# Moving a set of weight loads and their splits within the second of four batch groups

## The chip, the cores and the metric

The kernel runs on one core of a Trainium2 chip. The metric is device time in microseconds. One execution is also profiled; all rows below come from its trace, and their times count from the start of its span.

## What is computed

The input `x` is 32 samples of 64 channels and 1024 positions. Two layers follow each other, each with its own residual:

```
c  = conv(x, 9 taps, 4 channel groups) + (cond @ c_weight.T)[:, :, None] + bias
x  = x + c @ W.T + bias + (per-sample LoRA of c, rank 16)
m  = per-sample 64x64 mix of channels, weights = softmax(MLP(cond)) over 8 matrices
     applied to x, plus a mixed bias
s  = m @ Wr.T                      # 64 experts
G  = softmax over the 16 best of s, zero elsewhere
x  = x + 2 * ((m @ A_k.T) * G_k) @ B_k, summed over the 64 experts k, rank 16
```

With 64 experts of rank 16 the last line is two 1024x1024 products with the gates between them.

## The kernel before

The 32 samples are worked in four groups of eight (`g` = 0 to 3). A group has 512 tokens of 1024 elements, as four tiles of 128 rows. Every float32 matmul operand is split into a high part (a copy by ScalarE, `..._hi`) and a low part (the rest, a subtraction by VectorE, `..._lo`), and a product is three matmuls: high by high, high by low, low by high (`product`, L1374 to L1376).

Weights stream through four slots (`piece_hi`, `piece_lo`, piece n in slot n % 4). A piece of 512 KB comes in one of two ways. A *raw* piece is loaded to `raw` (two buffers) by SP (`next_raw`, L316), and split by ScalarE (L647) and VectorE (L893). Raw n can be loaded only when VectorE has split the raw piece two places before it. A *kept* piece was computed once, split, and stored in DRAM (`kept`); `fetch` loads both parts of it (L344, L345).

The first layer and the last product of groups 1 to 3 are done with seven block products instead of eight, and these need sums of weight blocks. There are four sets of such sums ("units" 0 to 3). For each, `load_weights` loads four blocks of 512 KB (L371), `combine` makes the sums in place on VectorE (L999 to L1006), `combined_hi` (ScalarE, L711) and `combined_lo` (VectorE, L1012) split them, and `keep_weights` stores each of the four splits with two DMAs of 512 KB (L378, L379). Sets 0 to 2 are made in group 0, set 3 in group 1, in the space of `conv_in` (the sums) and `u_hi`, `u_lo` (the splits). So `conv_in` can be loaded for group 2 only when the set's splits are done, and `u_hi` can take gated values of chunks c and c+1 only when the stores of that part have landed (`s_comb`).

A group goes through these stages on TensorE: the convolution (L1388), the first layer as products on pieces 0 to 13 with LoRA between them (L1395 to L1402), the mixing (L1408) and the scores (L1414, L1415) with the first h product among them, and the h stage. In the h stage product `h_of(c)`, here h0 to h7, uses raw piece 14 + c and writes one of the banks 2, 3, 6, 7, 4, 5, 2, 3. TensorE transposes the scores after the first part of h1 (`score_transposed`, L1431) and the gates after h2 (L1438). VectorE picks the 16 best (`choose`), and ScalarE stores the gates and spreads them back over the partitions, four DMAs of 256 KB (L699) ahead of split 21, four more as buffers come free. Then `gated` (L988) multiplies bank c by its gates; `u_hi`, `u_lo` take the split. After the h stage come products on pieces 22 to 35.

The order on each engine and queue is written out by hand, and each runs its own in order. In group 1, VectorE has the splits of raw pieces 17 to 21 and then the `gated` items, ScalarE has split 16, the exponentials of the gates, splits 17 and 18, the copy and store of the gates (`gates_out`), splits 19 and 20, `spread_gates`, split 21 and the gated chunks. SP has raw 16 and 17, the stores of set 3, raw 18, four loads of `conv_in` (L319), raw 19 to 21, two broadcasts of biases, raw 22. TensorE waits in h6 and h7 for the `gated` item that frees their bank:

```
if c >= 6 and ks[0] == 0:
    pe.wait_ge(s_item, g * ITEMS + H0 + c - 5)
```

Of the kernel before, what the change touches and what calls it, by code (L numbers as in the profile page):

```python
# [69 lines left out]
def adaln_ffn_kernel(nc, conv_x, x, taps, pieces, first_consts, hidden_w, later_consts, lora_a, lora_b,  # L70
                     starts, wr, expand, spread, out):
    with ExitStack() as ctx:
# [241 lines left out]
        def _(sp):  # L314
            def load_raw(r, piece):
                sp.dma_start(raw[:, r % RAWS, :], pieces[piece]).then_inc(s_raw[r % RAWS], 16)  # L316

            def load_conv_in(g, t):
                sp.dma_start(conv_in[:, 2 * t:2 * t + 2].rearrange("p b g q -> p (b g q)"),  # L319
                             conv_x[bass.ds(g, 1), t].rearrange("a p n -> (a p) n")).then_inc(s_convin[t], 16)  # L320
# [20 lines left out]
            def fetch(g, n):  # L341

                step_used(sp, g, n - SLOTS)
                sp.dma_start(piece_hi[:, n % SLOTS, :].bitcast(F32), kept[KEPT[n], 0]).then_inc(s_fetched[n % SLOTS], 16)  # L344
                sp.dma_start(piece_lo[:, n % SLOTS, :].bitcast(F32), kept[KEPT[n], 1]).then_inc(s_fetched[n % SLOTS], 16)  # L345

            def lo_done(r_lo):

                sp.wait_ge(s_piece_lo, r_lo)
# [129 lines left out]
            def group(g, last):  # L479
                def next_raw(n):  # L480

                    r = RAW_AT[n]
                    lo_done(g * RAWS_G + (3 + r))
                    load_raw(r, RAW[n % STEPS])

                fetch(g, 4)
                next_raw(8)
                fetch(g, 5)
                next_raw(9)
                if g == 1:  # L490
                    for i in range(4):
                        sp.wait_ge(s_comb_in[i], 48)
                        load_weights(3, i)
                fetch(g, 6)
                fetch(g, 7)
                next_raw(14)
                fetch(g, 10)
                next_raw(15)
                for n in range(11, 14):
                    fetch(g, n)  # L500
                next_raw(16)
                next_raw(17)
                if g == 1:
                    for step in range(4):
                        keep_weights(3, step)
                elif not last:
                    load_conv_in(g + 1, 0)
                    load_conv_in(g + 1, 1)
                next_raw(18)
                if g == 1:  # L510
                    load_conv_in(g + 1, 0)
                    load_conv_in(g + 1, 1)
                if not last:
                    load_conv_in(g + 1, 2)
                    load_conv_in(g + 1, 3)
                for n in range(19, 22):
                    next_raw(n)
                if not last:
                    cond_bias(g)
                    mix_bias(g)  # L520
                next_raw(22)
                next_raw(23)
                if g == 1:
                    for i in range(4):
                        sp.wait_ge(s_comb[i], 32 * 4)
                next_raw(26)
                next_raw(27)
                fetch(g, 24)
                fetch(g, 25)
                fetch(g, 28)  # L530
                next_raw(32)
                fetch(g, 29)
                fetch(g, 30)
                next_raw(33)
                fetch(g, 31)
                for t in range(2):
                    store(g, t, 0, 5 + t)
                if not last:
                    next_raw(STEPS)
                fetch(g, 34)  # L540
                if not last:
                    next_raw(STEPS + 1)
                fetch(g, 35)
                if not last:
                    next_raw(STEPS + 2)
                for t in range(2):
                    store(g, t, 1, 15 + t)
                if not last:
                    next_raw(STEPS + 3)
                    next_x(g, 0, 0)  # L550
                for t in range(2):
                    for h in range(2):
                        store(g, 2 + t, h, 21 + 2 * t + h if last else 18 + 3 * t + h)
                if not last:
                    for th, h in ((1, 1), (0, 1), (1, 0)):
                        next_x(g, th, h)

            first_group()
            for g in range(1, GROUPS):
                group(g, g == GROUPS - 1)  # L560
# [77 lines left out]
        def _(act):  # L638
# [51 lines left out]
            def gates_out(g, bank):  # L690
                act.wait_ge(s_gate_t, g + 1)
                act.activation(gate_t, banks[bank][0:KR_E, :], ACT.Copy).then_inc(s_gate_hi, 1)
                act.wait_ge(s_gate_hi, g + 1)
                act.dma_start(gates, gate_t).then_inc(s_gates_out, 16)
# [12 lines left out]
            def combined_hi(unit, step):  # L707

                i = (0, 1, 3, 2)[step]
                act.wait_ge(s_comb_sum, 4 * unit + step + 1)  # L710
                act.activation(kept_hi(unit, i), raw_weights(unit, i), ACT.Copy).then_inc(s_comb_hi, 1)  # L711
# [115 lines left out]
            def group(g, last):  # L827
                def next_split(n):

                    step_used(act, g, n - SLOTS)  # L830
                    split_raw(g, n)

                for b in range(GB):
                    conv_hi(g, b)
                    if b == 1:

                        act.wait_ge(s_conv, g * GB + 1)
                        split_raw(g, 3)
                first_product(g, 0, (4, 5))
                sums_hi(g, 0)  # L840
                lora_parts(g)
                next_split(8)
                next_split(9)
                next_split(14)
                next_split(15)
                for i, c in enumerate(CHUNKS):
                    split_hi(g, MIX0 + i, v_hi[:, c, :], work[:, c, :])
                    if g == 1 and i % 2 == 0:
                        combined_hi(3, i // 2)
                score_out(g, 5)  # L850
                next_split(16)
                gates_exp(g)
                next_split(17)
                next_split(18)
                gates_out(g, 0)
                next_split(19)
                next_split(20)
                act.wait_ge(s_gates_out, 16 * g + 16)
                for c in range(GATES):
                    spread_gates(c)  # L860
                next_split(21)
                for c in range(NCH):
                    if g == 1 and c % 2 == 0:
                        act.wait_ge(s_comb[c // 2], 32 * 4)
                    gated_hi(g, c)
                    if c == 1:
                        next_split(22)
                    if c == 3:
                        next_split(23)
                next_split(26)  # L870
                first_product(g, 1, (6, 7))
                next_split(27)
                sums_hi(g, 4)
                next_split(32)
                next_split(33)
                if not last:
                    next_split(STEPS)
                    next_split(STEPS + 1)
                    next_split(STEPS + 2)
# [6 lines left out]
        def _(dve):  # L886
            dve.wait_ge(s_ones, 4)

            def split_raw(g, n):

                r = RAW_AT[n]
                dve.wait_ge(s_piece_hi, g * RAWS_G + (5 + r))
                dve.tensor_tensor(piece_lo[:, n % SLOTS, :], raw[:, r % RAWS, :],  # L893
                                  piece_hi[:, n % SLOTS, :].bitcast(F32), ALU.subtract).then_inc(s_piece_lo, 1)
# [113 lines left out]
            def combined_lo(unit, step):  # L1008

                i = (0, 1, 3, 2)[step]  # L1010
                dve.wait_ge(s_comb_hi, 4 * unit + step + 1)
                dve.tensor_tensor(kept_lo(unit, i), raw_weights(unit, i), kept_hi(unit, i).bitcast(F32),  # L1012
                                  ALU.subtract).then_inc(s_comb_lo, 1)
# [160 lines left out]
            def group(g, last):  # L1174
# [102 lines left out]
                for i, c in enumerate(CHUNKS):  # L1277
                    mix_item(g, i, c, (6, 7, 4)[i % 3])
                    if i:
                        mix_lo(g, i - 1, CHUNKS[i - 1])  # L1280
                    if g == 1 and i % 2:
                        combined_lo(3, i // 2)
                mix_lo(g, NCH - 1, CHUNKS[-1])
                split_raw(g, 16)
                choose(g, 1)
                for n in range(17, 22):
                    split_raw(g, n)
                dve.wait_ge(s_lo, g * ITEMS + H0)
                for c in range(0, 6, 2):
# [509 lines left out]
```

## Time and profile before

| | us |
|---|---|
| median of three runs | 658.17 |
| lowest and highest | 656.51, 658.33 |
| the profiled execution | 656.7 |
| its span | 654.9 |
| TensorE busy | 648.1 (99%) |
| VectorE busy | 451.4 (69%) |
| ScalarE busy | 214.0 (33%) |
| DMA, mean rate | 241 GB/s |

Busy time of TensorE is modelled at the ends of matmuls, so 99% says that it has nearly no gaps. The mean granted clock is 0.999 of full speed. Group 1 runs from 178.8 to 337.6 us, group 2 from there to 494.5 us.

### The profile page before, as it was taken

The numbers are of one execution on the slowest core, as the hardware profiler recorded it, in microseconds if no ns is written. First come the engines' busy times: TensorE is split into PE (matmuls) and PEld (weight loads), VectorE is DVE, ScalarE is ACT, GpSimd is POOL, SyncE is SP. The second block draws the span as 40 slices with busy tenths as digits, with TensorE's granted clock in tenths as the row PEclk, the third lists the DMA queues.
The fourth block names the chain that finished last, engine by engine and source line by source line (L and its number), as shares of the span: only waits on it lengthen the run. The fifth ranks groups of instructions, "written<-read, shape, count | busy, mean of one in ns | idle before, by whom it ended". The sixth has DMA issues, their size and how long they took to land.

```text
span 654.9 us, 8354 instructions
## 1 busy us (share of the span) xinstructions
PE 648.1 (99%) x3197; PEld 537.7 (82%) x3197; DVE 451.4 (69%) x690; ACT 214.0 (33%) x275; POOL 73.8 (11%) x91
## 2 busy tenths in 40 slices
PE   9999999999999999999999999999999999999997
PEld 8878888888897788888889788888879888888885
DVE  2859469549377788558769758636967856665785
ACT  2714135233144024335115312333423421433420
POOL 1598200000000160000000042000000000000000
PEclk9999999999999999999999999999999999999999
DMA  8587714986969926776976682287797664037795
GB/s 303 210 293 279 299 50 144 356 246 218 392 228 379 356 100 260 280 223 245 366 275 220 261 318 97 102 225 245 290 325 264 273 248 184 0 118 203 211 345 221
DMA packets 51594, 157.98 MB, mean 241 GB/s; under 512 B 5488, under 2 KB 6384, under 8 KB 51568
## 3 DMA queue, kind: packets, MB, share of 16 engines
q1 hardware_dynamic: 46240, 148.05, 62.7%
q10 hardware_dynamic: 5328, 9.61, 4.8%
q8 instruction: 13, 0.21, 0.1%
q14 instruction: 13, 0.11, 0.1%
HBM read 131.94 MB, written 25.71 MB: 241 GB/s over the span
## 4 chain that ended last, share of the span: by engine, by line
PE 91%; DVE 3%; DMA 3%; issue 1%; SPq 1%; ACT 0%; DVEq 0%
PE bank L1374 25%; PE bank L1376 24%; PE bank L1375 24%; PE bank L1388 9%; PE bank L1408 3%; DMA piece_lo<-kept 2%; PE bank L1395 2%; PE bank L1414 1%; PE bank L1402 1%; PE bank L1400 1%; PE bank L1415 1%; DVE x L925 1%; DMA gate<-hidden_w 1%; DVE u_lo L1012 1%; DVE work L932 1%
## 5 line engine op out<-in xcount | busy, mean ns | idle before, releaser
L893 DVE TENSOR_TENSOR piece_lo<-raw,piece_hi 128x1024 fp32r<-128x1024 f32 x60 | 74.1, 1239 | 90.0 <-ACT piece_hi L647 89.8
L647 ACT ACTIVATE piece_hi<-raw 128x1024 fp32r<-128x1024 f32 x60 | 63.4, 1058 | 147.1 <-PE bank L1376 103.2
L1374 PE MATMUL bank<-piece_hi,u_hi 128*128 128x512 f32 x272 | 107.9, 397 | 0.0
L1376 PE MATMUL bank<-piece_hi,u_lo 128*128 128x512 f32 x272 | 107.3, 395 | 0.0
L1375 PE MATMUL bank<-piece_lo,u_hi 128*128 128x512 f32 x272 | 107.3, 394 | 0.0
L1374 PE MATMUL bank<-v_hi,piece_hi 128*128 128x512 f32 x256 | 101.8, 398 | 0.0
L1376 PE MATMUL bank<-v_hi,piece_lo 128*128 128x512 f32 x256 | 101.1, 395 | 0.0
L1375 PE MATMUL bank<-v_lo,piece_hi 128*128 128x512 f32 x256 | 101.0, 394 | 0.0
L1374 PE MATMUL bank<-piece_hi,v_hi 128*128 128x512 f32 x192 | 76.0, 396 | 0.8 <-DMA piece_lo<-kept 0.8
L1376 PE MATMUL bank<-piece_hi,v_lo 128*128 128x512 f32 x192 | 75.8, 395 | 0.0
L1375 PE MATMUL bank<-piece_lo,v_hi 128*128 128x512 f32 x192 | 75.8, 395 | 0.0
L652 ACT ACTIVATE u_hi<-work 128x512 fp32r<-128x512 f32 x64 | 40.1, 631 | 87.6 <-DVE work L988 50.8
L925 DVE TENSOR_TENSOR x<-x,bank 128x512 f32<-128x512 f32 x86 | 54.3, 679 | 17.0 <-PE bank L1402 12.7
L1374 PEld LDWEIGHTS bank<-piece_hi,u_hi 128*128 128x128 f32 x272 | 51.2, 188 | 12.4 <-issue 0.5
L1376 PEld LDWEIGHTS bank<-piece_hi,u_lo 128*128 128x128 f32 x272 | 51.2, 188 | 12.0
L1375 PEld LDWEIGHTS bank<-piece_lo,u_hi 128*128 128x128 f32 x272 | 51.2, 188 | 11.8
L1388 PE MATMUL bank<-toep,conv_in 128*128 128x128 f32 x512 | 59.2, 276 | 0.2 <-DMA toep<-taps 0.2
L1388 PEld LDWEIGHTS bank<-toep,conv_in 128*128 128x128 f32 x512 | 58.2, 192 | 0.8 <-DMA toep<-taps 0.4
L1376 PEld LDWEIGHTS bank<-v_hi,piece_lo 128*128 128x128 f32 x256 | 48.2, 188 | 11.5
L1375 PEld LDWEIGHTS bank<-v_lo,piece_hi 128*128 128x128 f32 x256 | 48.2, 188 | 11.0
L1374 PEld LDWEIGHTS bank<-v_hi,piece_hi 128*128 128x128 f32 x256 | 48.2, 188 | 10.9
L899 DVE TENSOR_TENSOR u_lo<-work,u_hi 128x512 fp32r<-128x512 f32 x64 | 43.7, 686 | 15.1 <-ACT u_hi L652 13.8
(143 smaller groups left out, 800.7 us busy)
## 6 DMA issues: line engine op xcount, KB each, us to landing
raw<-pieces SPq DMA_DIRECT2D x76, 512.0 KB, 5.5
piece_hi<-kept SPq DMA_DIRECT2D x48, 512.0 KB, 4.7
piece_lo<-kept SPq DMA_DIRECT2D x48, 512.0 KB, 5.8
x<-x SPq DMA_DIRECT2D x16, 512.0 KB, 5.3
gate_x<-gates ACTq DMA_DIRECT2D x32, 256.0 KB
out<-x SPq DMA_DIRECT2D x32, 256.0 KB, 4.8
conv_in<-conv_x SPq DMA_DIRECT2D x15, 516.0 KB, 7.1
conv_in<-pieces SPq DMA_DIRECT2D x12, 512.0 KB, 8.8
```

The costliest lines, as they stand in the source:

```text
L647: act.activation(piece_hi[:, n % SLOTS, :], raw[:, r % RAWS, :], ACT.Copy).then_inc(s_piece_hi, 1)
L652: act.activation(to, of, ACT.Copy).then_inc(s_hi, 1)
L893: dve.tensor_tensor(piece_lo[:, n % SLOTS, :], raw[:, r % RAWS, :], piece_hi[:, n % SLOTS, :].bitcast(F32), ALU.subtract).then_inc(s_piece ...
L899: dve.tensor_tensor(to, of, hi, ALU.subtract).then_inc(s_lo, 1)
L925: dve.tensor_tensor(half, half, of, ALU.add).then_inc(done, 1)
L932: dve.tensor_tensor(work[:, c, :], banks[bank][:, :], mixb_bc[:, :, :].rearrange("p b c -> p (b c)"), ALU.add).then_inc(s_item, 1)
L1374: pe.matmul(to, left_hi, right_hi, start=first, stop=False)
L1375: pe.matmul(to, left_hi, right_lo, start=False, stop=False)
L1376: return pe.matmul(to, left_lo, right_hi, start=False, stop=last)
L1388: mm = pe.matmul(banks[bank][:, cg * P:(cg + 1) * P], conv_in[:, b, cg, h:h + Q], toep[:, cg, 1 - h, :], start=(h == 0), stop=(h == 1))
L1395: mm = pe.matmul(banks[bank][0:LORA_M, :], lora_a_r[:, k, :], part[:, k, :], start=(k == 0 and part is u_hi), stop=(k == NCH - 1 and part ...
L1408: mm = pe.matmul(banks[bank][:, t * P:(t + 1) * P], x1[:, t, c * P:(c + 1) * P], blockdiag[:, t, :], start=True, stop=True)
```

## The change

In group 1, SP issues `fetch` 6 and 7 ahead of the four loads of set 3, no longer behind them. The splits of set 3 leave the mixing: `combined_hi` comes on ScalarE after split 18, ahead of `gates_out`, and `combined_lo` on VectorE after split 18, ahead of split 19. On SP the stores of set 3 follow them: raw 18, 19 and 20 go first, then the eight stores, then the four loads of `conv_in`, then raw 21. Groups 0, 2 and 3 keep their order.

```diff
@@ sp, group @@
                 next_raw(9)
+                fetch(g, 6)
+                fetch(g, 7)
                 if g == 1:
                     for i in range(4):
                         sp.wait_ge(s_comb_in[i], 48)
                         load_weights(3, i)
-                fetch(g, 6)
-                fetch(g, 7)
                 next_raw(14)
...
                 next_raw(17)
                 if g == 1:
+                    for n in range(18, 21):
+                        next_raw(n)
                     for step in range(4):
                         keep_weights(3, step)
-                elif not last:
-                    load_conv_in(g + 1, 0)
-                    load_conv_in(g + 1, 1)
-                next_raw(18)
-                if g == 1:
-                    load_conv_in(g + 1, 0)
-                    load_conv_in(g + 1, 1)
-                if not last:
-                    load_conv_in(g + 1, 2)
-                    load_conv_in(g + 1, 3)
-                for n in range(19, 22):
-                    next_raw(n)
+                    for t in range(4):
+                        load_conv_in(g + 1, t)
+                    next_raw(21)
+                else:
+                    if not last:
+                        load_conv_in(g + 1, 0)
+                        load_conv_in(g + 1, 1)
+                    next_raw(18)
+                    if not last:
+                        load_conv_in(g + 1, 2)
+                        load_conv_in(g + 1, 3)
+                    for n in range(19, 22):
+                        next_raw(n)
@@ act, group @@
                     split_hi(g, MIX0 + i, v_hi[:, c, :], work[:, c, :])
-                    if g == 1 and i % 2 == 0:
-                        combined_hi(3, i // 2)
...
                 next_split(18)
+                if g == 1:
+                    for step in range(4):
+                        combined_hi(3, step)
                 gates_out(g, 0)
@@ dve, group @@
                         mix_lo(g, i - 1, CHUNKS[i - 1])
-                    if g == 1 and i % 2:
-                        combined_lo(3, i // 2)
...
                 choose(g, 1)
-                for n in range(17, 22):
+                split_raw(g, 17)
+                split_raw(g, 18)
+                if g == 1:
+                    for step in range(4):
+                        combined_lo(3, step)
+                for n in range(19, 22):
                     split_raw(g, n)
```

## Rows read from the trace of the kernel before

**Rows 1.** The page, busy microseconds, share of the span and instructions of each engine.

```profile
PE 648.1 (99%) x3197; PEld 537.7 (82%) x3197; DVE 451.4 (69%) x690; ACT 214.0 (33%) x275; POOL 73.8 (11%) x91
```

**Rows 2.** TensorE's waits: who waited for what, us in total, times, longest.

```profile
PE bank L1374 <- DMA piece_lo<-kept: 0.8, 1, 0.8
PE bank L1414 <- DVE v_lo L899: 0.5, 2, 0.3
```

**Rows 3.** TensorE's timeline, groups 1, 2: start, us, instruction, idle before it.

```profile
204.10 0.40 PE L1395 MATMUL bank<-u_hi,lora_a_r 128*112 128x512 f32 x1
...
214.36 0.47 PE L1374 MATMUL bank<-piece_hi,v_hi 128*128 128x512 f32 x1 [0.79 <-DMA piece_lo<-kept]
...
363.01 0.39 PE L1395 MATMUL bank<-u_hi,lora_a_r 128*112 128x512 f32 x1
...
372.31 0.39 PE L1374 MATMUL bank<-piece_hi,v_hi 128*128 128x512 f32 x1
```

**Rows 4.** Windows of TensorE, mixing: length, busy (records), clock, DMA share, GB/s.

```profile
240.50:259.01 18.51, 17.90 (x108) 1.00 0.61 240
398.38:415.77 17.39, 17.39 (x108) 1.00 0.25 91
```

**Rows 5.** Timeline of SP's queue, first layer of group 1: start and us of the issue.

```profile
200.04 2.17 SPq L371 DMA_DIRECT2D conv_in<-pieces  x4
...
202.77 0.45 SPq L345 DMA_DIRECT2D piece_lo<-kept  x1
```

**Rows 6.** Windows of all engines: busy times, then clock, DMA share and GB/s.

```profile
198.46:213.56 15.10, 15.10 (x65) 11.67 (x64) 11.14 (x12) 6.81 (x8) 0.00 (x0) 1.00 1.02 406
...
277.00:279.40 2.40, 2.40 (x12) 1.97 (x11) 0.00 (x0) 0.00 (x0) 0.00 (x0) 1.00 0.99 306
279.40:290.00 10.60, 10.60 (x47) 8.57 (x47) 4.89 (x6) 3.39 (x4) 0.00 (x0) 1.00 0.82 229
```

**Rows 7.** TensorE's timeline: score transposes, first matmul of h6, first of product 22.

```profile
259.01 0.49 PE L1431 MATMUL bank<-consts,small 128*128 128x128 f32 x3
...
287.12 0.39 PE L1374 MATMUL bank<-v_hi,piece_hi 128*128 128x512 f32 x1
...
298.28 0.40 PE L1374 MATMUL bank<-piece_hi,u_hi 128*128 128x512 f32 x1
```

**Rows 8.** VectorE's timeline, h stage of group 1: splits 17, 18, 19, 20, first gated item.

```profile
266.38 2.35 DVE L893 TENSOR_TENSOR piece_lo<-raw,piece_hi 128x1024 fp32r<-128x1024 f32 x2
273.38 2.52 DVE L893 TENSOR_TENSOR piece_lo<-raw,piece_hi 128x1024 fp32r<-128x1024 f32 x2 [4.65 <-ACT piece_hi L647]
...
281.72 0.68 DVE L988 TENSOR_TENSOR work<-bank,gate_x 128x512 f32<-128x512 f32 x1
```

**Rows 9.** ScalarE's timeline in the same stage: copy of the gates, split 21.

```profile
270.59 0.59 ACT L692 ACTIVATE small<-bank 64x512 f32<-64x512 f32 x1 [5.20 <-PE bank L1438]
...
279.49 1.06 ACT L647 ACTIVATE piece_hi<-raw 128x1024 fp32r<-128x1024 f32 x1 [4.84 <-DMA raw<-pieces]
```

**Rows 10.** SP's queue in the same stage: loads of conv_in, raw 19 and 20, raw 21.

```profile
261.02 2.12 SPq L319 DMA_DIRECT2D conv_in<-conv_x  x4
267.62 1.46 SPq L316 DMA_DIRECT2D raw<-pieces  x2
...
274.64 0.33 SPq L316 DMA_DIRECT2D raw<-pieces  x1
```

**Rows 11.** Group 2: ScalarE's queue spreads the gates, VectorE's wait for the fourth.

```profile
430.44 2.52 ACTq L699 DMA_DIRECT2D gate_x<-gates  x4
...
447.85 0.69 DVE L988 TENSOR_TENSOR work<-bank,gate_x 128x512 f32<-128x512 f32 x1 [0.74 <-DMA gate_x<-gates]
```

**Rows 12.** Window of TensorE after its last matmul, columns as in rows 4.

```profile
652.00:654.90 2.90, 0.00 (x0) 0.86 0.68 251
```

**Rows 13.** TensorE's timeline: the first matmuls of the kernel, the convolution of group 3.

```profile
0.99 5.09 PE L1370 MATMUL bank<-ones 128*128 128x128 f32 x24 [0.99 <-POOL ones L566]
...
494.30 14.45 PE L1388 MATMUL bank<-toep,conv_in 128*128 128x128 f32 x128
```

## Prediction

> **What bounds the kernel now.** I read the page's busy times first: TensorE is busy for 99% of the span [rows 1], so nothing but its own work and its few stalls sets the end. The change touches no matmul. It can give back stalls, or make new ones. The waits of TensorE come next: one wait on a transfer, of `piece_lo<-kept`, lasts 0.8 us [rows 2]; the others are smaller and lie at the start or in the mixing.
>
> The four groups run one after another, and groups 1 and 2 issue the same matmuls, so group 2 is a ruler for group 1. From the first LoRA matmul to the start of product 6 to 7, TensorE's timeline has 214.36 - 204.10 = 10.26 us in group 1 and 372.31 - 363.01 = 9.30 us in group 2 [rows 3]: 0.96 us lost, in one place. From the first mixing matmul to the score transposes it is 18.51 us against 17.39 us, both of 108 records [rows 4]: 1.12 us lost. This is all that the change can win, 2.1 us or 0.3% (about what a measurement of this kernel can tell from no change).
>
> **Part 1, the loads go behind fetches 6 and 7.** The issues on SP's queue show the stall's cause. Four loads of 512 KB are issued at 200.04 us, the low half of piece 6 at 202.77 us [rows 5], and it is used at 214.36 us, 11.6 us later. In this stretch the queue moves 406 GB/s [rows 6], so 512 KB (0.524 MB) take 1.29 us and the four loads 5.2 us. Without them in front, piece 6 lands some 5 us earlier, against a need of 0.96 us. The stall goes whole. Next in line is piece 7, which loses its four predecessors too. The loads themselves then land in the place of the two fetches, at about 217 us; the sums that read them (L999) come on VectorE at 222 us, a cover of some 4 us. If it were gone, VectorE and not TensorE would wait first. Gain 0.96 us.
>
> **Part 2, the mixing loses four splits.** VectorE has four `combined_lo` between the mix items, and the scores wait for its `v_lo` there, two waits of 0.5 us in sum and the rest spread over slower steps [rows 2]. ScalarE's four `combined_hi` leave with them. Group 2 without them shows the gain, 1.12 us. Part of it may stay lost: the first of the two waits lies ahead of all four splits, behind work that isn't changed. I take 0.94 us, between 0.7 and 1.1. Parts 1 and 2 together: -1.9 us (1.7 to 2.1).
>
> **Part 3, the splits in the h stage.** I count from M, the start of the score transposes, 259.01 us in group 1 [rows 7]. VectorE ends the splits of pieces 17 and 18 at 266.38 + 2.35 = M+9.7 and starts that of 19 at 273.38 = M+14.4 [rows 8]. Four splits at 2.35 / 2 = 1.18 us take 4.7 us, from M+9.7 to M+14.4. They fill the idle time exactly and delay piece 19 by nothing, which TensorE needs only for h5, one h product of 5.6 us ahead of h6, at M+22.5 [rows 7]. The four on ScalarE lie ahead of its copy of the gates, where it idles 5.20 us for TensorE's transposes [rows 9]. So the engines' work costs 0, with a cover of 7 us on TensorE's side once split 19 is done.
>
> **Part 4, what the moved step puts on SP's queue.** This is where I expect the time to go. Each of the four steps also issues two stores of 512 KB (`kept`). Before, these eight ran in the mixing, ahead of raw 18. Now they come behind raw 20, and the four loads of conv_in, which ran at 261.02 us [rows 10], follow them; raw 21 is put behind all twelve. Before, raw 21 was issued at 274.64 us = M+15.6 and its split began on ScalarE at 279.49 us, 4.85 us later [rows 9, 10]. Now SP waits for the fourth `combined_lo` (M+14.4), issues two stores (0.9 us) and four loads (2.12 us [rows 10]), and issues raw 21 at M+17.4. That is 1.8 us later, but what counts is the queue in front of it.
>
> Raw 19 and 20 are issued at 267.62 us [rows 10] and are in at about M+14, when VectorE takes them up [rows 8]. The stores begin to issue at M+10.9, so from M+14 the queue has work without a gap: 8 x 0.524 + 4 x 0.528 + 0.524 (raw 21) = 6.83 MB.
> - At 406 GB/s [rows 6] that is 16.8 us: raw 21 lands at M+30.8. This is the lower end, no longer stretch shows this queue faster.
> - But from M+15 on ScalarE's queue spreads the gates: four copies of 256 KB, 1.05 MB. In group 2 their issue began at 430.44 us and VectorE stopped waiting for the fourth at 447.85 us, 17 us later [rows 11], so they are slow and share the DMA engines until about M+32. In the 2.4 us where raw 21 and these copies run together, both queues move 306 GB/s; over 279.4 to 290 us it is 229 GB/s [rows 6]. With 306, M+15 to M+32 moves 5.2 MB, 4.15 MB of it SP's; 0.4 MB went before, and the last 2.28 MB take 5.6 us: M+37.6. With 229 it is 3.9 - 1.05 = 2.85 MB, then 3.58 MB or 8.8 us: M+40.8, the upper end (that stretch has gaps without work, so I stay nearer to 306).
> I take M+37.5.
>
> **Who waits for raw 21.** VectorE's program has split 21 ahead of the first `gated`. From landing to `gated` on chunk 0 pass one ScalarE split, one VectorE split and the item itself: 281.72 + 0.68 - 279.49 = 2.9 us [rows 8, 9], and 3.0 us with TensorE's start. Product h6 writes bank 2, the bank of h0, and waits for that very item (`s_item` of H0+1). Before, this was ready at M+23.4, and h6 started at 287.12 us = M+28.1 [rows 7]: 4.7 us of slack, and no wait is seen. Now it is ready at M+40.6: TensorE stands for 12.5 us (5.7 to 15.8).
>
> **The clock.** In the window after the last matmul the granted clock is 0.86 in the mean [rows 12]: with nothing left to do, TensorE falls from its level of 2.4 to that of 1.2 GHz. A stall of 12 us will do this too. At the start, 24 records of 128x128 took 5.09 us, 212 ns each, where the conv's 128 take 14.45 us, 113 ns each [rows 13]; the start lost 24 x 99 ns = 2.4 us by running at half speed (the form isn't quite the same, so it is an estimate). I take 2.3 us for h6 after the stall, 1.5 to 3.
>
> **What is late next.** Product 22 starts 11.2 us after h6 [rows 7] and needs chunks 0 to 3 gated, product 24 another 5.6 us later needs all eight. VectorE's chain from chunk 0 to there holds waits for gates that will have landed long before, and the half clock gives it 2 us more. Raw 22 comes behind two small broadcasts and raw 21, at M+42 to M+46, against a need at M+54. I cost it at 0, with up to 1 us in the upper end.
>
> **Sum.** -1.9 + 12.5 + 2.3 = +12.9 us. The profiled execution took 656.7 us (span 654.9), 1.5 us under the median of the three runs, 658.17; such executions lie at 656.5 or 658.3. I start from the middle of the four, 657.4 us, and get 670.3 us.
>
> **The rivals.**
> - *Short stall*: the gates' copies don't slow SP's queue. For it speaks that they move few bytes. Raw 21 lands at M+30.8, stall 5.7 us, clock 1.5 us: +5.3 us, 662 to 663 us.
> - *No stall, faster*: transfers of one queue pass each other, or spread so that a late one isn't held by those ahead. Raw 21 then takes its 4.85 us from issue, is in at M+22.3 and h6 is ready at M+25.3, before M+28.1. What is left is -1.9 us: 655.5 us. It decides if raw 21 lands before M+25.1. Against it: piece 6's low half took 11.6 us behind four loads [rows 3, 5], about what 3.7 MB in front of it need at 406 GB/s, while raw 21 with an empty queue took 4.85 us.
> - *Stall carried on*: gating the later chunks is late for products 22 and 24 as well, up to 5 us more: over 675 us.
> - *The change doesn't do what it says*: the moved loads or splits leave the old stalls. That is 2 us at most and is lost in the range.
>
> The Trainium skill speaks for the second rival: "DMA: Bandwidth & Descriptors", section "Queues, rings and completion order", says that completion isn't first in, first out for one issuing engine, and that only the start of descriptors keeps its order on each DMA engine. Taken as licence for raw 21 to overtake, the sum would be -1.9 us; taken as order of starts on every engine, it is that of part 4. The trace bears out the latter by the 11.6 us named above.
>
> **How the numbers follow.** Forecast (stall 8 to 16 us with clock) 0.71; short stall 0.15; no stall 0.07; carried on 0.07. The range takes the lower end from 656.7 + 5.3 = 662.0 us and the upper from 658.2 + 15.8 + 3 - 1.7 = 675.3 us, and leaves out the second rival and most of the last. Slower by over 0.3%: 0.92. The no-stall case gives 0.29%, right at the bound, so its 0.07 is split: faster 0.04, within 0.04.
>
> **What would show it.** Part 1: no wait of TensorE for `piece_lo<-kept` in group 1. Part 2: 17.4 to 17.7 us from mixing to transposes. Part 3: split 19 within 0.5 us of M+14.4. Part 4: an idle gap of TensorE ahead of h6, put down to VectorE's `work` item, preceded by ScalarE waiting 15 us or more for `raw<-pieces`; a granted clock below 1 after it. I am wrong if ScalarE's split 21 starts before M+25, or if the gap is there but well under 8 us, in which case the queue was faster under the gates' copies than I read.

## The result and the profile after

The changed kernel takes 671.8 us (median of 5 runs, 670.7 to 673.3) against 657.6 us before (median of 5 too, 656.5 to 658.3): a ratio of 1.022, 95% interval 1.020 to 1.024. The forecast was 670.3 us. The profiled execution is the longest of the five, 673.3 us with a span of 671.5 us, 16.6 us over that of before. Line numbers from here on are those of each kernel's own file; in the changed one the products are L1381 to L1383, the ScalarE split of a raw piece L650, VectorE's L897, and the gated item L992.

TensorE's waits, in the columns of rows 2. The 0.8 us for `piece_lo<-kept` are gone, one of the two score waits is left, and there is one new wait of 15 us. The waits for `ones` and `toep` lie ahead of everything that was changed:

```profile
PE bank L1381 <- DVE work L992: 15.0, 1, 15.0
PE bank L1377 <- POOL ones L569: 1.0, 1, 1.0
PE bank L1395 <- DMA toep<-taps: 0.5, 1, 0.5
PE bank L1421 <- DVE v_lo L903: 0.3, 1, 0.3
```

The mixing of group 1, in the columns of rows 4, takes 17.64 us where it took 18.51 us. The DMA engines are at 31 GB/s there, no longer at 240:

```profile
240.38:258.02 17.64, 17.39 (x108) 1.00 0.09 31
```

M, the score transposes, is now at 258.02 us. Then comes the h stage. SP's queue, to be read against rows 10. The last store is issued at 276.57 us and raw 21 at 282.74 us = M+24.7:

```profile
269.14 0.33 SPq L378 DMA_DIRECT2D kept<-u_hi  x1
...
273.93 1.36 SPq L379 DMA_DIRECT2D kept<-u_lo  x1
275.33 1.19 SPq L378 DMA_DIRECT2D kept<-u_hi  x1
276.57 1.26 SPq L379 DMA_DIRECT2D kept<-u_lo  x1
277.87 4.82 SPq L319 DMA_DIRECT2D conv_in<-conv_x  x4
282.74 0.50 SPq L316 DMA_DIRECT2D raw<-pieces  x1
```

VectorE and ScalarE in the same stage, against rows 8 and 9: the four splits of set 3, the splits of pieces 19 and 20, then a wait of 24 us for raw 21, and the gated item right behind its split:

```profile
267.89 4.63 DVE L1016 TENSOR_TENSOR u_lo<-conv_in,u_hi 128x1024 fp32r<-128x1024 f32 x4
272.44 1.22 DVE L897 TENSOR_TENSOR piece_lo<-raw,piece_hi 128x1024 fp32r<-128x1024 f32 x1
273.96 1.23 DVE L897 TENSOR_TENSOR piece_lo<-raw,piece_hi 128x1024 fp32r<-128x1024 f32 x1 [0.31 <-ACT piece_hi L650]
299.50 1.23 DVE L897 TENSOR_TENSOR piece_lo<-raw,piece_hi 128x1024 fp32r<-128x1024 f32 x1 [24.31 <-ACT piece_hi L650]
300.65 1.28 DVE L992 TENSOR_TENSOR work<-bank,gate_x 128x512 f32<-128x512 f32 x2
```

```profile
276.03 5.41 ACTq L702 DMA_DIRECT2D gate_x<-gates  x4
298.42 1.06 ACT L650 ACTIVATE piece_hi<-raw 128x1024 fp32r<-128x1024 f32 x1 [24.48 <-DMA raw<-pieces]
```

TensorE then. h6 begins at 301.39 us = M+43.4 instead of M+28.1. Its matmuls follow each other in 0.43 us and, from about 307.5 us, in 0.23 us again:

```profile
301.39 0.80 PE L1381 MATMUL bank<-v_hi,piece_hi 128*128 128x512 f32 x1 [15.05 <-DVE work L992]
...
305.39 0.63 PE L1381 MATMUL bank<-v_hi,piece_hi 128*128 128x512 f32 x1
305.82 0.63 PE L1382 MATMUL bank<-v_lo,piece_hi 128*128 128x512 f32 x1
...
307.49 0.40 PE L1383 MATMUL bank<-v_hi,piece_lo 128*128 128x512 f32 x1
307.72 0.40 PE L1381 MATMUL bank<-v_hi,piece_hi 128*128 128x512 f32 x1
```

And the windows of TensorE, in the columns of rows 4 (length, busy and records, granted clock, DMA share, GB/s). Both queues together move 384 GB/s up to 282 us and then 311, 284 and 205 GB/s. The granted clock falls to half within the gap and is half for 6 us after it:

```profile
276.00:282.00 6.00, 6.00 (x28) 1.00 1.03 384
282.00:288.00 6.00, 4.34 (x19) 1.00 1.02 311
288.00:294.00 6.00, 0.00 (x0) 0.70 1.04 284
294.00:298.40 4.40, 0.00 (x0) 0.50 0.60 205
301.40:307.50 6.10, 6.10 (x15) 0.51 0.71 234
```

### The profile page after: what moved, and what is told of

Same layout as the page of the kernel before. It is cut to its first block, busy times and chain, and to the rows that moved or that the text cites. A ratio compares the mean times of both kernels' runs of the same rounds, so it can differ in the third digit from the quotient of the medians.

```text
span 671.5 us, 8354 instructions
## 1 busy us (share of the span) xinstructions
PE 650.6 (97%) x3197; PEld 540.4 (80%) x3197; DVE 450.8 (67%) x690; ACT 214.5 (32%) x275; POOL 73.3 (11%) x91
## 3 DMA queue, kind: packets, MB, share of 16 engines
q10 hardware_dynamic: 5328, 9.61, 4.6%
## 4 chain that ended last, share of the span: by engine, by line
PE 89%; DVE 3%; DMA 3%; SPq 1%; issue 1%; ACT 1%; ACTq 0%; DVEq 0%
PE bank L1381 23%; PE bank L1382 23%; PE bank L1383 23%; PE bank L1395 9%; PE bank L1415 4%; DMA raw<-pieces 2%; PE bank L1402 2%; PE bank L1421 1%; PE bank L1422 1%; DMA toep<-taps 1%; PE bank L1407 1%; PE bank L1409 1%; DVE x L929 1%; SPq L319 1%; DVE u_lo L1016 1%
## 5 line engine op out<-in xcount | busy, mean ns | idle before, releaser
L897 DVE TENSOR_TENSOR piece_lo<-raw,piece_hi 128x1024 fp32r<-128x1024 f32 x60 | 73.9, 1239 | 107.9 <-ACT piece_hi L650 107.9
L1381 PE MATMUL bank<-v_hi,piece_hi 128*128 128x512 f32 x256 | 103.1, 403 | 15.0 <-DVE work L992 15.0
L650 ACT ACTIVATE piece_hi<-raw 128x1024 fp32r<-128x1024 f32 x60 | 63.3, 1059 | 166.9 <-PE bank L1383 102.8
L1381 PE MATMUL bank<-piece_hi,u_hi 128*128 128x512 f32 x272 | 107.9, 397 | 0.1
L1383 PE MATMUL bank<-piece_hi,u_lo 128*128 128x512 f32 x272 | 107.3, 394 | 0.0
L1383 PE MATMUL bank<-v_hi,piece_lo 128*128 128x512 f32 x256 | 102.0, 399 | 0.0
L1383 PE MATMUL bank<-piece_hi,v_lo 128*128 128x512 f32 x192 | 75.8, 395 | 0.0
L1381 PE MATMUL bank<-piece_hi,v_hi 128*128 128x512 f32 x192 | 75.8, 395 | 0.0
L1381 PEld LDWEIGHTS bank<-v_hi,piece_hi 128*128 128x128 f32 x256 | 48.8, 191 | 26.7 <-DVE work L992 15.5
L1381 PEld LDWEIGHTS bank<-piece_hi,u_hi 128*128 128x128 f32 x272 | 51.2, 188 | 12.4 <-issue 0.6
L1383 PEld LDWEIGHTS bank<-piece_hi,u_lo 128*128 128x128 f32 x272 | 51.2, 188 | 12.0
L1383 PEld LDWEIGHTS bank<-v_hi,piece_lo 128*128 128x128 f32 x256 | 48.8, 191 | 11.8
L903 DVE TENSOR_TENSOR u_lo<-work,u_hi 128x512 fp32r<-128x512 f32 x64 | 43.4, 687 | 15.5 <-ACT u_hi L655 14.3
```

The source lines that it names most:

```text
L650: act.activation(piece_hi[:, n % SLOTS, :], raw[:, r % RAWS, :], ACT.Copy).then_inc(s_piece_hi, 1)
L903: dve.tensor_tensor(to, of, hi, ALU.subtract).then_inc(s_lo, 1)
L1381: pe.matmul(to, left_hi, right_hi, start=first, stop=False)
L1383: return pe.matmul(to, left_lo, right_hi, start=False, stop=last)
```

## The experiments

### The loads alone

```diff
@@ sp, group (against the kernel before) @@
+                fetch(g, 6)
+                fetch(g, 7)
                 if g == 1:
...
                         load_weights(3, i)
-                fetch(g, 6)
-                fetch(g, 7)
```

> The kernel before with part 1 alone: in group 1 fetch 6 and 7 are issued ahead of the four loads of set 3; all splits and stores stay in the mixing. My theory: TensorE's wait for piece_lo<-kept goes and nothing follows it, 0.96 us less, ratio 0.9985 (about 656.6 us). Rival, a stall moves on: the later loads make the sums on VectorE late and the time stays at 657.5 us with a new wait of about 1 us on VectorE's chain. Rival, the moved loads are what made the changed kernel slow: then over 660 us.

Measured: 656.7 us against 657.5 us, a ratio of 0.9987 (0.9976 to 0.9999). The wait for `piece_lo<-kept` is gone, and 0.4 us of another has come in group 1, in the convolution, ahead of everything that was moved:

```profile
PE bank L1414 <- DVE v_lo L899: 0.6, 2, 0.3
PE bank L1388 <- DMA toep<-taps: 0.4, 1, 0.4
PE bank L1388 <- DVE work L903: 0.4, 1, 0.4
```

Part 1 removes the stall that it was meant to remove. Its size, 0.96 us, fits the ratio, but the interval nearly reaches 1, so the gain in time is only just seen. The wait for `work` isn't in the profile of the changed kernel, which has the same loads, and is in that of other kernels below, so it belongs to the execution and not to the loads.

### The splits and stores alone

```diff
@@ sp, group (against the changed kernel) @@
                 next_raw(9)
-                fetch(g, 6)
-                fetch(g, 7)
                 if g == 1:
...
                         load_weights(3, i)
+                fetch(g, 6)
+                fetch(g, 7)
```

> The changed kernel with part 1 undone: the four loads of set 3 are again ahead of fetch 6 and 7, splits and stores of set 3 stay in the h stage. My theory: the wait for piece_lo<-kept of 0.8 us is back, the gap ahead of h6 is the same 15 us, the time 1 us over the changed kernel, 672 to 674 us, ratio to before 1.023. Rival (the loads' place is part of the loss): under 668 us.

Measured: 673.4 us, ratio 1.0245 (1.021 to 1.028). The gap ahead of h6 is 15.0 us again. The ratio lies over the 1.022 of the changed kernel, as expected, but the intervals overlap, so the difference isn't shown. The old stall is back too, but shorter: from the first LoRA matmul to product 6 TensorE takes 214.33 - 204.72 = 9.61 us, 0.3 us over the 9.30 us of group 2 in rows 3, not 0.96 us.

```profile
204.72 0.39 PE L1402 MATMUL bank<-u_hi,lora_a_r 128*112 128x512 f32 x1
...
213.79 0.40 PE L1383 MATMUL bank<-piece_hi,v_lo 128*128 128x512 f32 x1
214.33 0.47 PE L1381 MATMUL bank<-piece_hi,v_hi 128*128 128x512 f32 x1
```

So its size differs between two executions with the same order of loads. The gap ahead of h6 has nothing to do with part 1.

### The stores alone, no engine work moved

```diff
@@ act and dve, group (against the changed kernel): the splits back in the mixing @@
+                    if g == 1 and i % 2 == 0:
+                        combined_hi(3, i // 2)
...
+                    if g == 1 and i % 2:
+                        combined_lo(3, i // 2)
...
@@ ... and out of the h stage @@
-                        combined_hi(3, step)
...
-                        combined_lo(3, step)
```

> All splits of set 3 in the mixing as before, part 1 in place, but SP's queue in the order of the changed kernel: raw 18 to 20, the eight stores, the four loads of conv_in, raw 21. It has no engine work moved, only the transfers. My theory: the whole loss is here, a gap of 13 to 15 us ahead of h6 and 2.8 us of half clock, and the 0.9 us of the mixing is lost again: 671 to 674 us. Rival (the moved splits on VectorE and ScalarE make a good part of the loss): under 667 us.

Measured: 671.9 us, ratio 1.023 (1.021 to 1.025). TensorE's waits:

```profile
PE bank L1377 <- DVE work L991: 14.1, 1, 14.1
```

The mixing is back at 18.57 us, and the gap is there with no split of set 3 in the h stage. So the transfers make the loss, and the four splits on VectorE and ScalarE none that can be seen.

### Raw 21 ahead of the loads, ahead of the stores, and without the loads

```diff
@@ sp, group, g == 1 (against the changed kernel): c_raw21_before_conv @@
                         keep_weights(3, step)
+                    next_raw(21)
                     for t in range(4):
                         load_conv_in(g + 1, t)
-                    next_raw(21)
@@ d_raw21_first: raw 21 ahead of the stores @@
-                    for n in range(18, 21):
+                    for n in range(18, 22):
                         next_raw(n)
...
-                    next_raw(21)
@@ e_conv_late: as d, and the loads behind raw 23 @@
-                    for t in range(4):
-                        load_conv_in(g + 1, t)
...
                 next_raw(23)
                 if g == 1:
+                    for t in range(4):
+                        load_conv_in(g + 1, t)
```

> The changed kernel, but raw 21 is issued ahead of the four loads of conv_in, still behind the eight stores. My theory (the queue holds raw 21): in the changed kernel the last store was in at M+27, so raw 21 lands at about M+29.5 instead of M+40.4, h6 is ready at M+32.5 and the gap ahead of it falls from 15 to 4 or 5 us; raw 22 is now held instead and adds up to 3 us ahead of product 22. In all 661 to 666 us. Rival (the splits of set 3 on VectorE and ScalarE delay the gates, the queue doesn't matter): unchanged at 671 to 673 us.

> The changed kernel, but raw 21 is issued ahead of the eight stores too, with the four loads of conv_in behind the stores. My theory: raw 21 lands by M+21, h6 has no gap. The queue then holds raw 22, which comes behind all twelve transfers at about M+40; its split sits in VectorE's order ahead of chunks 2 and 3, so product 22, due at M+39.3, waits 5 to 8 us, with 2 to 3 us of half clock: 662 to 667 us. Rival (only raw 21 matters): 655.7 us. Rival (engine work of the splits): unchanged at 671 to 673 us.

> The changed kernel, but raw 21 is issued ahead of the eight stores, and the four loads of conv_in go behind raw 23. Loads and splits of set 3 stay where the change put them. My theory (the change's parts 1 to 3 are sound and only the order on SP's queue is not): raw 22 comes behind the stores at M+31 to M+33, in time for product 22; no gap ahead of h6 or product 22, the full 1.9 us is gained: ratio 0.997, 655.7 us. Rival (the splits in the h stage cost something themselves): 657.5 us or more. Rival (conv_in is late for group 2): a wait of TensorE for conv_in at the start of group 2.

Measured: 669.8 us (ratio 1.0185, 1.017 to 1.020), 671.6 us (1.020, 1.018 to 1.023) and 667.7 us (1.018, 1.015 to 1.020). All three are slower than I expected (661 to 666, 662 to 667 and 655.7 us), the last by 12 us. Their waits of TensorE, in this order:

```profile
PE bank L1381 <- DVE work L992: 5.3, 1, 5.3
PE bank L1381 <- DVE u_lo L903: 4.9, 2, 3.9
```

```profile
PE bank L1380 <- DVE u_lo L902: 13.3, 1, 13.3
```

```profile
PE bank L1380 <- DVE u_lo L902: 6.9, 1, 6.9
PE bank L1380 <- DMA piece_lo<-kept: 1.7, 1, 1.7
```

With raw 21 ahead of the loads the gap ahead of h6 is 5.3 us, as expected, but 4.9 us, 3.9 of them ahead of product 22, come behind it. TensorE waits 4.8 us less than in the changed kernel and the time falls by only 2 us. Part of the rest is the clock, which fell twice: it is 0.50 from 292.4 to 297 us, behind the first gap, and 0.61 from 309.7 to 314 us, behind the second. With raw 21 first, h6 waits for nothing, and product 22 waits 13.3 us: raw 22, now behind the twelve transfers, is late in its place, and its split stands in VectorE's order ahead of chunks 2 and 3. With the loads away too, ScalarE's timeline shows what is left:

```profile
279.59 1.06 ACT L649 ACTIVATE piece_hi<-raw 128x1024 fp32r<-128x1024 f32 x1 [5.89 <-DMA raw<-pieces]
284.06 0.63 ACT L654 ACTIVATE u_hi<-work 128x512 fp32r<-128x512 f32 x1 [3.41 <-DMA kept<-u_lo]
...
298.94 1.06 ACT L649 ACTIVATE piece_hi<-raw 128x1024 fp32r<-128x1024 f32 x1 [13.62 <-DMA raw<-pieces]
```

Raw 21 is in at 279.59 us (M+21.8, M being 257.84 us there), chunk 0 waits 3.4 us for the stores of its own part to land, and raw 22 is in at 298.94 us, M+41 and not M+31 to M+33. SP's queue and the windows of TensorE (columns of rows 4) show two reasons that I had left out:

```profile
273.88 0.60 SPq L378 DMA_DIRECT2D kept<-u_hi  x1
```

```profile
257.84:268.00 10.16, 10.16 (x47) 1.00 0.21 60
268.00:278.00 10.00, 10.00 (x46) 1.00 0.66 184
278.00:288.00 10.00, 10.00 (x44) 1.00 1.02 406
```

The first store goes out at M+16.0; in the changed kernel it went out at M+11.1. SP issues in the order of its program, and raw 21, now ahead of the stores, can't be issued before VectorE has ended split 19, at M+15.6, and so freed the buffer. So the DMA engines are busy for only 0.66 of the time from M+10 to M+20. Then the eight stores run beside the gates' copies, and they take longer: 22.0 us from the first issue to the last landing (273.88 us to 280.28 us plus 15.6 us), against 15.8 us in the changed kernel (269.14 us to 276.57 us plus 8.4 us). The theory (the queue holds what comes last) stands, but neither of these two orders is the cure. Whether the h stage has room for these transfers in some other order stays open, since the engines stood partly idle up to M+20.

### The gates' copies cut to a quarter

```diff
@@ act, group (against the changed kernel) @@
                 for c in range(GATES):
-                    spread_gates(c)
+                    if g == 1:
+                        spread_quarter(c)
+                    else:
+                        spread_gates(c)
```

`spread_quarter` copies 128 of the 512 columns and leaves the gates of the other columns as they were, so this kernel doesn't compute the right result. It is for timing alone.

> The changed kernel, but in group 1 the first four copies that spread the gates move a quarter of the columns (128 of 512), so the gates of these chunks are wrong there; all else is as in the changed kernel. It prices what ScalarE's queue takes from SP's. My theory: raw 21 lands at M+31 to M+34 instead of M+40.4, the gap ahead of h6 is 6 to 9 us instead of 15, the time 662 to 665 us. Rival (the copies are small and SP's queue is slow for another reason, such as stores and loads mixed): raw 21 stays at M+38 or later, 669 us or more.

Measured: 666.4 us, ratio 1.014 (1.011 to 1.017). ScalarE's split of piece 21 and TensorE's h6:

```profile
291.33 1.06 ACT L650 ACTIVATE piece_hi<-raw 128x1024 fp32r<-128x1024 f32 x1 [18.66 <-DMA raw<-pieces]
```

```profile
294.30 0.80 PE L1389 MATMUL bank<-v_hi,piece_hi 128*128 128x512 f32 x1 [9.33 <-DVE work L1000]
```

M is 256.65 us there, so raw 21 is in at M+34.7 instead of M+40.4. Copies that lost 0.8 MB gave back 5.7 us, where 0.8 MB at 406 GB/s are 1.9 us: here they cost SP's queue three times their bytes.

The traces also show when they do. In `e_conv_late`, from 278 to 288 us, SP's queue has the stores, ScalarE's moves 0.74 MB of the gates' copies, and both together reach 406 GB/s. In `i_splits_behind_mix` below, from 270 to 274 us, SP's queue alone has the loads of conv_in and raw pieces and moves 407 GB/s. In the changed kernel, from 284 to 294 us, loads of conv_in run beside 0.49 MB of copies, and both together reach 285 GB/s; with the small gates, from 284 to 290 us, it is 378 GB/s. So in these windows stores beside the copies lose nothing and loads beside them lose about 30%. Why isn't shown.

### Staying in the mixing, but later in it

```diff
@@ act, group (against the kernel with the loads alone) @@
-                    if g == 1 and i % 2 == 0:
-                        combined_hi(3, i // 2)
+                    if g == 1 and i >= 4:
+                        combined_hi(3, i - 4)
@@ dve, group: f_splits_late_mix @@
-                    if g == 1 and i % 2:
-                        combined_lo(3, i // 2)
+                    if g == 1 and i in (5, 7):
+                        combined_lo(3, (i - 5) // 2)
                 mix_lo(g, NCH - 1, CHUNKS[-1])
+                if g == 1:
+                    combined_lo(3, 2)
+                    combined_lo(3, 3)
```

`i_splits_behind_mix` puts all four `combined_lo` behind the last `mix_lo`. `j_late_mix_conv_late` is the first of the two with the four loads of conv_in behind raw 23.

> The kernel before with part 1, and the splits of set 3 moved within the mixing instead of out of it: ScalarE's four go behind its last four v_hi, VectorE's two behind items 5 and 7 and two behind the last v_lo, where group 2 shows VectorE idle for 3.5 us. The stores and loads of conv_in keep their place on SP's queue, ahead of raw 19. My theory (VectorE's place in the first half of the mixing costs the 0.9 us, and the stores must run while the DMA engines have room, at 91 GB/s in group 2's mixing): mixing of 17.4 to 17.7 us, no gap in the h stage, 1.9 us under before: 655.5 us, ratio 0.997. Rival (stores two microseconds later already hold raw 18 to 21): a new gap, over 657.5 us.

> As f_splits_late_mix, but all four of VectorE's splits stand behind the last v_lo, ahead of split 16 and the choice of the 16 best. They take 4.6 us where 3.5 are free, so the choice ends 1.2 us later, still 3 us ahead of the gates' transposes; the eight stores begin around M and raw 18 comes behind them, raw 21 lands at about M+26 and h6 is ready at M+29 against M+28.1. My theory: between no gap and 2 us: 655.5 to 658 us. Rival (the queue's order decides nothing until the gates' copies run): the same as f_splits_late_mix.

> As f_splits_late_mix, with the four loads of conv_in behind raw 23 instead of ahead of raw 19. In f_splits_late_mix raw 21 was in at M+23.5, 1.6 us ahead of the time at which h6 would wait, and 4 of its 12 executions were 3 us longer than the rest. My theory: those executions crossed that point; with the loads gone from the queue raw 19 to 21 land 1 to 4 us earlier, no execution is longer, and the gain of up to 1.9 us holds: 655.5 us, ratio 0.997 to 0.999. Rival (the longer executions have another cause): they are still there.

Measured: 656.6 us (1.001, 0.9996 to 1.003), 660.0 us (1.004, 1.002 to 1.006) and 662.3 us (1.009, 1.006 to 1.012).

The first has a mixing of 17.65 us, no gap, and a group 1 of 157.8 us in its profile where before had 158.8 us. But 4 of its 12 executions lie at 659.6 to 660.2 us and the rest at 655.7 to 657.1 us, and in the mean nothing is gained. Three of the four long ones have a mean granted clock of 0.997, the rest 0.998 to 1.000. A short gap ahead of h6 with half clock behind it would give that, but no long execution was profiled. The second has a gap of 3.6 us ahead of h6: its stores begin as the mixing ends, and raw 18 to 21 come behind them. Its h6:

```profile
289.21 0.50 PE L1375 MATMUL bank<-v_hi,piece_hi 128*128 128x512 f32 x1 [3.61 <-DVE work L988]
```

The third has raw 21 in early (M+19), and TensorE waits ahead of product 24, for piece 24:

```profile
PE bank L1376 <- DMA piece_lo<-kept: 4.8, 1, 4.8
```

The loads of conv_in now run beside the gates' copies. VectorE waits 4.5 and 4.0 us for copies, its split of piece 23 ends late, SP can issue raw 27 only at 297.46 us and the low half of piece 24 at 298.30 us, which lands 9.5 us later, at 307.83 us. VectorE's last gated chunk, also held by a copy, ends at 307.81 us, so getting the piece in earlier would not have been enough. Its executions lie at 661.4 to 666.3 us, so it can't say whether the longer executions of the first came from raw 21. That stays open.

## Why the prediction was right

**What bounds the kernel.** TensorE's waits and the span move together: group 1 grew by 16.0 us, which is the 15.3 us by which h6 is later and 2.8 us of half clock, less 1.9 us gained, to 0.2 us; 0.9 us more lie ahead of group 1 and 0.4 us less behind it, where nothing was changed.

**Parts 1 and 2.** Forecast -1.9 us. From the start of group 1 to M it took 259.01 - 178.66 = 80.35 us before and takes 258.02 - 179.57 = 78.45 us: -1.90 us. The mixing gave 0.87 us (0.94 expected), since the first score's wait stayed, as the text had allowed.

**Part 3.** VectorE's four splits took 4.63 us, and split 19 began at 272.44 us = M+14.42; M+14.4 was forecast. `h_stores_moved_only`, which has the same time without them in the h stage, shows that they cost nothing that can be seen.

**Part 4, right in mechanism and small in size.** Raw 21 was in at M+40.4, not M+37.5, near the upper end of M+40.8. Two terms of the sum were mis-sized. The gates' copies were to run from M+15 to about M+32. They began at 276.03 us = M+18.0, since the store of the gates itself took 5.8 us to land beside SP's stores (2.6 us before), and ended only around M+40: ScalarE's queue still moved 0.26 MB from 294 to 298.4 us and nothing from there to 301 us. And the rate, put at 306 GB/s up to M+32 and at 406 GB/s behind it, went the other way: 384 GB/s up to 282 us = M+24, while stores went, then 311, 284 and 205 GB/s, while the loads of conv_in and raw 21 ran beside the copies. The two errors of the rate partly cancel, since the mean from 271 to 298.4 us is 320 GB/s; what was too fast is the 406 GB/s of the last 5.6 us. Also, raw 21 was issued at M+24.7, not M+17.4: SP's issues took 1.2 to 1.6 us each once the queue was deep (0.3 to 0.5 us in rows 5 and 10). By the windows that made little difference, since the DMA engines' share was 1.02 to 1.04 from 282 to 294 us with what stood in front; no run tests it.

**Who waits for raw 21.** The chain from ScalarE's split to h6 was put at 3.0 us. In six kernels h6 begins 2.97 us after the start of that split: 298.42 and 301.39 us in the changed one, 291.33 and 294.30 us with the small gates, 289.42 and 292.39 us with raw 21 ahead of the loads, 286.24 and 289.21 us with the splits behind the mixing, and likewise in the two others with this gap. The point from which it decides, raw 21 in at M+25.1, is bracketed: at M+23.6 no gap (`f_splits_late_mix`), at M+28.9 one of 3.6 us (`i_splits_behind_mix`).

**The clock.** Put at 2.3 us (1.5 to 3), it cost 2.8 us: product 22 starts 315.38 - 301.39 = 13.99 us after h6, where rows 7 have 11.16 us. The row of the kernel's start gave a fair size.

**What is late next.** Nothing, as costed: product 22 follows h6 and h7 without a wait, and no fetch is late.

**Sum.** 12.5 + 2.3 - 1.9 = 12.9 us were forecast, 14.3 us is the difference of the medians. (M+37.5 and 3.0 us make M+40.5, so 12.4 us would have been the stall of that sum.) The profile's 16.6 us is of the longest execution.

**The rivals.** The second one, no stall because transfers pass each other, is out: raw 21 came as late as the work in front of it, and every move of it on the queue moved its landing, from M+40.4 to M+30.7 ahead of the loads and to M+22.6 and M+21.8 ahead of the stores. That is the reading of the Trainium skill's page "DMA: Bandwidth & Descriptors", section "Queues, rings and completion order", in which descriptors of one queue start in order on each DMA engine, and the trace agrees with it (15.7 us from issue to use, against 4.85 us before). Landings do change places by a little: in `e_conv_late` a store issued at 277.61 us was in after 8.9 us, ahead of the one issued at 276.27 us, which took 11.6 us. The 3.7 MB that the prediction puts in front of piece 6's low half take 9.1 us at 406 GB/s, not 11.6 us, so that argument was weaker than these moves are. The short stall is out by the small gates: even with a quarter of these copies it was 9.3 us.

Where I was wrong is in the cures. I priced `e_conv_late` at 655.7 us with raw 22 in at M+31 to M+33, and it was in at M+41. A transfer that is let pass makes the next in line late, and by more than I had reckoned: after each step forward the wait was at the next user of the queue. And I had overlooked that a transfer which must wait for a free buffer holds up all that SP issues behind it.

## What to carry to other kernels

Splits that are moved take their stores with them, and the stores take the buffers' next loads. Before moving an engine's work into its idle time, look at what the DMA engines do there: here the mixing had room for 4.2 MB, and the h stage, where loads and the gates' copies run side by side, had not enough where it was needed. Sum the bytes on the queue up to the first transfer that something waits for, at the rate that both queues reach together, and then do it again for the next one; a transfer let past the queue is paid for by the one behind it. Look also at what each issue waits for, since the engines may stand idle behind one that waits for a buffer.

## What the runs showed of the hardware

- Small copies on one queue can cost loads on the other more than their bytes: 0.8 MB less of gate copies brought raw 21 in 5.7 us earlier. Loads beside these copies and the copies moved 285 GB/s together (changed kernel, 284 to 294 us), loads alone 407 GB/s (`i_splits_behind_mix`), and stores with such copies 406 GB/s (`e_conv_late`).
- SP's issue of a DMA takes longer when its queue is deep: 1.2 to 1.6 us for a store that took 0.3 to 0.4 us with an empty one.
- In the changed kernel the granted clock fell from 1.00 to 0.50 within the gap and came back 6 us after work went on. A short gap costs clock too: with the splits behind the mixing, TensorE stood for 3.6 us at full clock, and the fall came as it went on, with 11 matmuls in 4.0 us and then 18 in 3.8 us; the windows are the gap, the 4 us behind it, and the next:

```profile
285.60:289.20 3.60, 0.01 (x1) 1.00 0.79 245
289.20:293.20 4.00, 3.99 (x11) 0.57 0.73 251
293.20:297.00 3.80, 3.80 (x18) 1.00 0.67 235
```

- The stall that part 1 removes was 0.96 us in one profile (before) and 0.3 us in another with the same order of loads (`b_splits_only`), so a stall of this size, read from one trace, can be off by 0.6 us.
